# A gated attention and feed-forward block on one core: another order of the opening, the first maxima spread by TensorE, and small moves in the loop

## The chip, the cores and the metric

The kernel runs on 1 core of a Trainium2 chip. The metric is the device time of one execution, in microseconds (us); less is better.

## The reference

For each of 16 batches `x` is 256 x 512 and `ctx` 256 x 512. A gated attention with 8 heads of 64 is added to `x`, then a feed-forward part with quantised weights and activations:

```python
log_D = log_fg_matrix + ig.T                      # lower triangle, -inf elsewhere
max_log_D = jnp.max(log_D, axis=-1, keepdims=True)
D = jnp.exp(log_D - max_log_D)
C = (q @ (k.T / sqrt(DH))) * D
normalizer = jnp.maximum(jnp.abs(C.sum(-1, keepdims=True)), jnp.exp(-max_log_D))
h = C / (normalizer + EPS) @ v                    # then an RMS norm per head

def weight_quant(w):                              # one scale for a whole weight
    scale = 1.0 / jnp.clip(jnp.mean(jnp.abs(w)), EPS, None)
    return jnp.clip(jnp.round(w * scale), -1.0, 1.0) / scale

g, u = bitlinear(x, w_gate), bitlinear(x, w_up)   # 512 -> 2048
h = jnp.square(jax.nn.relu(g)) * u
return bitlinear(h, w_down)                       # 2048 -> 512

x = x + jnp.tanh(g_xattn[0]) * attention(layernorm(x), ctx, ctx, gates...)
x = x + jnp.tanh(g_ffn[0]) * ffn(layernorm(x), w_gate, w_up, w_down)
```

## The kernel before

Each engine has a program written out by hand, and they meet in semaphores. `step(b, n, m, par)` does the feed-forward part of batch b, the heads of batch n = b+1 and the gates of batch m = b+2; step 0 is written out, steps 1 to 12 run in a loop of two, and steps 13, 14 (no m) and 15 (no n) are written out too. In front of step 0 stands the opening: gates of batches 0 and 1, heads of batch 0, and the quantisation of the gate and up weights.

*Weights.* Each of `w_gate`, `w_up`, `w_down` comes as four pieces of 128 x 2048 (1 MB) into two buffers `stage`, gate and down in the first, up in the second. `magnitudes` (L506 on ScalarE, L739 on VectorE) sums a piece's absolute values, `weight_total` (L1077) and `weight_scale` (L729 to L734) make the scale `winv`, and `wprod` (L978, L980) the products of scales. Then a piece is multiplied and shifted by a magic number (L422 on GpSimd, L511 on ScalarE) and turned ternary, by a sign on ScalarE (L516) or by two roundings on VectorE (L745, L748). The down weight goes through all of this within step 0, the other two in the opening, where GpSimd scales all their pieces and VectorE rounds the four up pieces.

*Gates and maxima.* `gate_products` (L1164), `gates_in`, `forget_gate`, `log_forget` and `cumulative_sum` (L1174) give the sums; `cumulative` on VectorE writes `csum` and `a` (L842, L843); `a_rows` on TensorE transposes `a` (L1180), `running_max` scans it to `mrow` (L848). `spread_max` on SP stores `mrow` to memory (L358) and loads it back into `dmat`, on all 128 partitions (L364). `exponentials` on ScalarE work on `dmat` in place (L564, L570), `masks` on GpSimd (L429) cut the triangle, `scores` (L1124, L1125) and `weigh` on VectorE (L862) multiply, `heads_out` (L1137) gives the heads in the one bank `tp`, and `heads` on ScalarE (L578) copies each pair out.

*After the heads.* `normaliser` (L870 on), `head_squares` (L883), `mean_squares`, `head_rms`, `scale_heads` (L900), `residual` (L908, second half on GpSimd L436), `token_stats` (L915), `tokens_rstd`, `token_centres` (L925, L928), `quantise_tokens` (L935 to L945), `token_columns` on TensorE (L1198), `tokens` on ScalarE (L551).

*Feed-forward.* `chunk(b,t,c)` is the gate half (4 matmuls into `gb`) and the up half (4 into `ub`), L1090; `relu_square` L524 and L526; `hidden` on VectorE L755; `hidden_max` L762 and L767; `hidden_scale` L777 to L782; quantisation L788 and L544; `hidden_transposes` L1104; `hidden_cols` L538 and L796; `down` L1116 in two halves; `output` on VectorE L805. `keep_warm` (L1204) are matmuls whose result nobody reads.

In the loop TensorE runs `cumulative_sum`, the gate half of chunk (b,1,0), `a_rows`, and the up half; VectorE runs `scale_heads`, `output(b-1,1)`, `cumulative`, `residual`, `running_max`, `token_stats`, `hidden(b,1,0)`.

## Time and profile before

| | |
|---|---|
| three runs | 636.77, 637.5, 637.85 us; median 637.5 |
| the profiled execution | 638.38 us, of which span 636.7 us |
| mean granted TensorE clock | 0.965 |
| TensorE busy | 578.6 us (91%) |
| VectorE busy | 526.7 us (83%) |
| ScalarE busy | 454.3 us (71%) |
| GpSimd busy | 129.9 us (20%) |

The span runs from the first to the last instruction. In the rows PE is TensorE's matmuls, DVE VectorE, ACT ScalarE, POOL GpSimd and SPq the queue of SP, which only issues DMAs; L12 is line 12 of the kernel before. A timeline row is start, duration, engine, line, operation, output<-inputs, shapes and count, and in square brackets how long the engine had been idle and what released it. Rows are merged where an engine repeats.

### The profile page before, as it was taken

How to read it: one execution, taken by the hardware profiler on the slowest of the kernel's cores; microseconds unless marked ns; L12 is line 12 of the kernel's file. 1: busy time of each engine (PE TensorE's matmuls, PEld its weight loads, DVE VectorE, ACT ScalarE, POOL GpSimd, SP SyncE). 2: the span in 40 equal slices, each digit the busy share in tenths (PEclk: the TensorE clock that was granted, in tenths of full speed). 3: DMA queues.
4: the chain of work that ended last, by engine and by line, in shares of the span. 5: the costliest groups of instructions: out<-in, count | busy, mean ns of one | idle time of the engine just before them, and what ended most of it. 6: DMA issues, size and time to landing. Idle time of an engine off the chain costs nothing.

```text
span 636.7 us, 18420 instructions
## 1 busy us (share of the span) xinstructions
PE 578.6 (91%) x6596; PEld 338.0 (53%) x6596; DVE 526.7 (83%) x1144; ACT 454.3 (71%) x925; POOL 129.9 (20%) x266
## 2 busy tenths in 40 slices
PE   7592768999999999999999999999999999999896
PEld 4361443656555564656555565646565555656442
DVE  4479595898989989898989899898989899897964
ACT  5374979858685877858686868768586868677662
POOL 1256240212121202112121202021121212021200
PEclk9785968999999999999999999999999999999998
DMA  9884505041140505050320505050412305020000
GB/s 311 306 287 139 192 2 167 18 140 62 43 159 17 182 0 199 0 182 17 103 95 19 179 8 191 0 187 11 156 43 77 121 17 183 3 100 1 34 19 33
DMA packets 45169, 63.73 MB, mean 100 GB/s; under 512 B 1872, under 2 KB 26704, under 8 KB 45136
## 3 DMA queue, kind: packets, MB, share of 16 engines
q1 hardware_dynamic: 45136, 63.30, 28.8%
q8 instruction: 20, 0.33, 0.2%
q14 instruction: 13, 0.11, 0.1%
HBM read 54.77 MB, written 8.52 MB: 99 GB/s over the span
## 4 chain that ended last, share of the span: by engine, by line
PE 59%; DVE 17%; issue 10%; ACT 6%; DMA 5%; DVEq 1%; POOL 1%; SPq 0%; ACTq 0%; POOLq 0%
PE ub L1090 15%; PE gb L1090 14%; PE yb L1116 10%; PE ab L1124 6%; PE tp L1137 5%; PE ab L1104 3%; DVE ssq L883 3%; DMA stage<-in_w_up 2%; PE ab L1125 2%; DVE stage L805 2%; DMA xs<-in_x 2%; DVE stage L755 1%; DMA max_rows<-mrow 1%; PE ab L1198 1%; DVE dmat L862 1%
## 5 line engine op out<-in xcount | busy, mean ns | idle before, releaser
L1090 PE MATMUL ub<-wuT,xqT 128*128 128x512 bf16 x512 | 133.1, 383 | 2.0 <-DVE stage L755 2.0
L1090 PE MATMUL gb<-wgT,xqT 128*128 128x512 bf16 x512 | 133.3, 383 | 1.5 <-ACT xqT L551 1.5
L524 ACT ACTIVATE relu<-gb 128x512 f32<-128x512 f32 x128 | 75.4, 589 | 77.3 <-PE gb L1090 75.1
L1116 PE MATMUL yb<-wdT,stage 128*128 128x512 bf16 x512 | 122.8, 384 | 3.6 <-ACT stage L538 3.6
L755 DVE TENSOR_TENSOR stage<-relu,ub 128x512 f32<-128x512 f32 x128 | 87.0, 680 | 26.6 <-ACT relu L526 26.1
L862 DVE SCALAR_TENSOR_TENSOR dmat<-ab,dmat 128x384 f32<-128x384 f32 x128 | 65.3, 551 | 31.7 <-POOL dmat L429 22.7
L526 ACT ACTIVATE relu<-relu 128x512 f32<-128x512 f32 x128 | 80.7, 631 | 4.1
L1090 PEld LDWEIGHTS ub<-wuT,xqT 128*128 128x128 bf16 x512 | 50.3, 99 | 61.2 <-DVE stage L755 3.0
L1116 PEld LDWEIGHTS yb<-wdT,stage 128*128 128x128 bf16 x512 | 47.4, 99 | 53.4 <-issue 4.7
L1090 PEld LDWEIGHTS gb<-wgT,xqT 128*128 128x128 bf16 x512 | 46.0, 100 | 49.9 <-ACT xqT L551 1.8
L429 POOL TENSOR_SCALAR_AFFINE_SELECT dmat<-dmat 128x256 f32<-128x256 f32 x128 | 55.3, 461 | 68.0 <-ACT dmat L570 67.9
L1137 PE MATMUL tp<-values,dmat 128*64 128x65 f32 x1536 | 60.4, 229 | 3.6 <-issue 3.6
L1137 PEld LDWEIGHTS tp<-values,dmat 128*64 128x64 f32 x1536 | 51.5, 141 | 15.9 <-issue 10.8
L1124 PE MATMUL ab<-qT,cT 64*128 64x256 f32 x256 | 52.7, 437 | 5.4 <-DVE dmat L862 5.4
L570 ACT ACTIVATE dmat<-dmat,a 128x256 f32<-128x256 f32 x128 | 57.3, 496 | 0.0
L762 DVE TENSOR_REDUCE stage<-stage 128x1 f32<-128x1536 f32 x32 | 56.0, 1749 | 0.1
L459 POOL TENSOR_SCALAR dq<-hm,wprod 128x1 f32<-128x1 f32 x32 | 9.1, 284 | 222.8 <-DVE rhm L780 217.7
L564 ACT ACTIVATE dmat<-dmat,a 128x128 f32<-128x128 f32 x128 | 43.7, 391 | 7.0 <-DMA dmat<-max_rows 7.0
L436 POOL TENSOR_TENSOR x<-ysq,xs 128x512 f32<-128x512 f32 x16 | 28.4, 1774 | 82.4 <-DVE stage L805 78.3
L544 ACT ACTIVATE hq<-stage,hqs 128x1024 f16<-128x1024 f32 x32 | 36.7, 1146 | 5.7 <-DVE hqs L782 5.7
L578 ACT ACTIVATE ysb<-tp 128x260 f32<-128x260 f32 x64 | 24.5, 382 | 22.5 <-PE tp L1137 22.5
L1124 PEld LDWEIGHTS ab<-qT,cT 64*128 64x128 f32 x256 | 24.8, 188 | 26.5 <-issue 19.3
(110 smaller groups left out, 870.8 us busy)
## 6 DMA issues: line engine op xcount, KB each, us to landing
dmat<-max_rows SPq DMA_DIRECT2D x16, 1024.0 KB, 5.1
values<-in_ctx_v SPq DMA_DIRECT2D x16, 520.0 KB, 7.7
xs<-in_x SPq DMA_DIRECT2D x16, 512.0 KB, 5.9
cT<-in_ctx_t SPq DMA_DIRECT2D x16, 512.0 KB, 6.9
out<-stage SPq DMA_DIRECT2D x32, 256.0 KB, 2.0
stage<-in_w_gate SPq DMA_DIRECT2D x4, 1024.0 KB, 12.7
stage<-in_w_up SPq DMA_DIRECT2D x4, 1024.0 KB, 11.1
stage<-in_w_down SPq DMA_DIRECT2D x4, 1024.0 KB, 5.6
```

The costliest lines, as they stand in the source:

```text
L429: nc.gpsimd.affine_select(out=dv, in_=dv, compare_op=ALU.is_ge, fill=0.0, base=0, pattern=[[0, 2], [1, P]], channel_multiplier=-1).then_in ...
L524: nc.scalar.activation(relu[:, c % 2, :], gb[c % 2][:, :], ACT.Relu).then_inc(g_free, 1)
L526: nc.scalar.activation(relu[:, c % 2, :], relu[:, c % 2, :], ACT.Square).then_inc(r2_ready, 1)
L564: nc.scalar.activation(dmat[:, hd, 2, :], dmat[:, hd, 1, :], ACT.Exp, bias=a[npar][:, 1, hd:hd + 1], scale=-1.0).then_inc(e_low, 1)
L570: last = nc.scalar.activation(dh, dh, ACT.Exp, bias=a[npar][:, 0, hd:hd + 1], scale=-1.0)
L755: nc.vector.tensor_tensor(h[t][:, c * CH:(c + 1) * CH], relu[:, c % 2, :], ub[c % 2][:, :], ALU.mult).then_inc(h_done, 1)
L762: nc.vector.tensor_reduce(h[t][:, FF:FF + 1], h[t][:, 0:3 * CH], axis=AX_X, op=ALU.max, apply_absolute_value=True).then_inc(quant_step, 1)
L862: nc.vector.scalar_tensor_tensor(dh, ab[hd % 2][:, 0:3 * P], HD ** -0.5, dh, ALU.mult, ALU.mult).then_inc(a_free[hd % 2], 1)
L1090: last = nc.tensor.matmul(bank[c % 2][:, :], xqT[par][:, t, d, :], w[:, d, c * CH:(c + 1) * CH], start=(d == 0), stop=(d == KD - 1))
L1116: done = nc.tensor.matmul(yb[:, :], hqT[:, c, :], wdT[:, c, :], start=(c == 0), stop=(c == KF - 1))
L1124: nc.tensor.matmul(ab[e][:, 0:S], cT[npar][rows, kd, 0:P], qT[npar][rows, kd, 0:S], start=True, stop=True)
L1137: done = nc.tensor.matmul(tp[rows, (2 * t + e) * VW:(2 * t + e + 1) * VW], dmat[:, hd, block, rows], values[npar][:, s, hd, :], start=firs ...
```

## The change

*The opening.* The maxima of batch 0 no longer go through memory. A 0/1 matrix `pick` (8 x 1024, laid over a buffer that is free then) selects one row of `mrow` for each head, so that 8 matmuls `spread_max` write the rows on all partitions into the banks of `gb` and `ub`; ScalarE's `first_exponentials` read them there. The fillers of `keep_warm` go to `yb` for that time, and their counts change. The gates of batch 1 move behind the heads of batch 0 on TensorE, ScalarE and VectorE. SP's loads come in another order. `magnitudes` are dealt out anew between ScalarE and VectorE (gate pieces as before; up: ScalarE 0, 2 and 3; down: ScalarE 0 and 1, VectorE 2 and 3).

*Scaling.* GpSimd scales a piece in four instructions of 512 columns, all gate pieces (the third and fourth only after `wprod`) and down pieces 0 and 1. VectorE scales all up pieces and down pieces 2 and 3; ScalarE scales none. ScalarE makes up pieces 0 and 1 ternary by the sign, VectorE rounds pieces 2 and 3, now in step 0. Gate pieces 2 and 3 get their sign in step 0. The second residual half of batch 0 goes from GpSimd to VectorE.

*The loop.* On TensorE both halves of chunk (b,1,0) stand ahead of `a_rows`. On VectorE `cumulative` stands ahead of `output(b-1,1)`. In step 14 `hidden(b,1,0)` stands ahead of `token_stats`; in step 15 the fourth chunk stands ahead of the whole of `down`, and `output(b,0)` behind the last quantisation.

The diff, cut:

```diff
+        pick = hq[0][0:NH, :].bitcast(F32)
...
+        spread_rows = [gb[0], gb[1], ub[0], ub[1]]
...
-            for n in range(2):
-                keys(n, n)
-            weights(0, w_gate, 0, 4)
+            queries(0, 0)
+            keys(0, 0)
+            queries(1, 1)
+            weights(0, w_gate, 0, 2)
             padded_values(0, 0)
-            spread_max(0, 0)
+            weights(0, w_gate, 2, 4)
+            keys(1, 1)
             weights(1, w_up, 0, 4)
             padded_values(1, 1)
+            weights(2, w_down, 0, 1)
             spread_max(1, 1)
-            weights(2, w_down, 0, 4)
+            weights(2, w_down, 1, 2)
             load(2, 0)
+            weights(2, w_down, 2, 4)
...
 
                 gp.wait_ge(winv_step, WINV[m])
-                w = weight_piece(m, i)
-                nc.gpsimd.tensor_scalar(w, w, winv[:, m:m + 1], MAGIC32, ALU.mult, ALU.add).then_inc(w_scaled[m], 1)
+                for k in range(KD):
+                    w = weight_piece(m, i)[:, CH * k:CH * (k + 1)]
+                    last = nc.gpsimd.tensor_scalar(w, w, winv[:, m:m + 1], MAGIC32, ALU.mult, ALU.add)
+                last.then_inc(w_scaled[m], 1)
 
             def masks(n, p):
...
                 alone(gp, gp_passed)
                 nc.gpsimd.tensor_scalar(dq[:, t:t + 1], hm1[:, t:t + 1], wprod[:, 2:3], 0.0, ALU.mult, ALU.add).then_inc(dq_ready, 1)
 
+            for p in range(NP):
+                masks(0, p)
             scale_weight(0, 0)
-            masks(0, 0)
-            masks(0, 1)
             scale_weight(0, 1)
-            masks(0, 2)
-            masks(0, 3)
+            gp.wait_ge(winv_step, WINV[1] + 2)
             scale_weight(0, 2)
+            token_factor(0, 0)
             scale_weight(0, 3)
-            scale_weight(1, 0)
-            residual(0, 0)
-            for i in range(1, 4):
-                scale_weight(1, i)
-            token_factor(0, 0)
             masks(1, 0)
 
...
+            def first_exponentials(p):
+
+                act.wait_ge(rows_spread, p + 1)
+                for e in range(2):
+                    hd = 2 * p + e
+                    nc.scalar.activation(dmat[:, hd, 2, :], spread_rows[p][:, e * S + P:(e + 1) * S], ACT.Exp,
+                                         bias=a[0][:, 1, hd:hd + 1], scale=-1.0).then_inc(e_low, 1)
+                for e in range(2):
+                    hd = 2 * p + e
+                    last = nc.scalar.activation(dmat[:, hd, 0:2, :].rearrange("p c s -> p (c s)"),
+                                                spread_rows[p][:, e * S:(e + 1) * S], ACT.Exp,
+                                                bias=a[0][:, 0, hd:hd + 1], scale=-1.0)
+                last.then_inc(e_done, 1)
...
-            attention_rstd(1)
             forget_gate(0)
             magnitudes(0, 0, 0)
+            attention_rstd(1)
+            for p in range(NP):
+                first_exponentials(p)
+            heads(0, 0)
+            exp_minus_max(0, 0)
+            magnitudes(0, 2, 1)
+            for p in range(1, NP):
+                heads(0, p)
+            squares(0)
...
                     log_forget(m)
                 if n is not None:
                     scale_heads(n)
+                if m is not None:
+                    cumulative(m, par)
                 if prev:
                     output(b - 1, 1, npar)
-                if m is not None:
-                    cumulative(m, par)
                 if n is not None:
                     residual(n, npar)
                 if m is not None:
                     running_max(m, par)
+                else:
+                    hidden(b, 1, 0)
                 if n is not None:
                     token_stats(n, npar)
-                hidden(b, 1, 0)
+                if not prev:
+                    scale_weight(2, 2)
+                if m is not None:
+                    hidden(b, 1, 0)
                 if n is not None:
                     token_centres(n, npar)
+                if not prev:
+                    scale_weight(2, 3)
                 hidden(b, 1, 1)
...
-                output(b, 0, par)
+                if n is not None:
+                    output(b, 0, par)
                 hidden_scale(b, 1, par)
                 quantise_low(b, 1)
+                if n is None:
+                    output(b, 0, par)
...
-            def keep_warm(count):
+            def spread_max(p):
+
+                if p == 0:
+                    pe.wait_ge(tp_free, gate_use(0, A_ROWS) + 1)
+                for e in range(2):
+                    hd = 2 * p + e
+                    done = nc.tensor.matmul(spread_rows[p][:, e * S:(e + 1) * S], pick[:, hd * P:(hd + 1) * P], mrow[:, :],
+                                            start=True, stop=True)
+                done.then_inc(rows_spread, 1)
...
+            keep_warm(2, yb)
+            spread_max(0)
+            spread_max(1)
             scores(0, 0, 0)
             scores(0, 1, 0)
-            max_columns(1)
-            keep_warm(6)
-            weight_total(0)
+            spread_max(2)
+            spread_max(3)
+            max_columns(0)
+            keep_warm(1, yb)
...
-            keep_warm(6)
+            weight_total(0)
+            q_columns(1, 1)
+            gate_products(1, 1, 0, T * 2 * KD)
+            keep_warm(6, ub[1])
+            cumulative_sum(1)
+            a_rows(1, 1)
+            keep_warm(6, ub[1])
             weight_total(1)
-            keep_warm(24)
+            max_columns(1)
+            keep_warm(20, ub[1])
             token_columns(0)
...
-                chunk(b, 1, 0, par, 0, 1)
+                chunk(b, 1, 0, par)
                 if m is not None:
                     a_rows(m, par)
-                chunk(b, 1, 0, par, 1, 2)
                 chunk(b, 1, 1, par)
                 hidden_transposes(b, 0)
                 chunk(b, 1, 2, par)
                 if m is not None:
                     max_columns(m)
-                down(b, 0, 0, KF // 2)
-                chunk(b, 1, 3, par)
-                if n is not None:
+                if n is not None:
+                    down(b, 0, 0, KF // 2)
+                    chunk(b, 1, 3, par)
                     token_columns(n)
-                down(b, 0, KF // 2, KF)
+                    down(b, 0, KF // 2, KF)
+                else:
+                    chunk(b, 1, 3, par)
+                    down(b, 0, 0, KF)
```

TensorE in the loop, from `down` of the batch before to the second chunk, before:

```order
L1116 MATMUL yb<-wdT,stage 128x512 x8
...
L1174 MATMUL tp<-logf,upper 128x16
L1175 MATMUL tp<-logf,ones 128x8
...
L1090 MATMUL gb<-wgT,xqT 128x512 x4
...
L1180 MATMUL tp<-ident,a 8x128 x2
L1090 MATMUL ub<-wuT,xqT 128x512 x4
...
L1090 MATMUL gb<-wgT,xqT 128x512 x4
L1090 MATMUL ub<-wuT,xqT 128x512 x4
```

and in the change:

```order
L1181 MATMUL yb<-wdT,stage 128x512 x8
...
L1239 MATMUL tp<-logf,upper 128x16
L1240 MATMUL tp<-logf,ones 128x8
...
L1155 MATMUL gb<-wgT,xqT 128x512 x4
L1155 MATMUL ub<-wuT,xqT 128x512 x4
...
L1245 MATMUL tp<-ident,a 8x128 x2
...
L1155 MATMUL gb<-wgT,xqT 128x512 x4
L1155 MATMUL ub<-wuT,xqT 128x512 x4
```

The transposes of `a` moved from between the two halves of the chunk to behind them.

VectorE in the loop, from `scale_heads` (`ysq`) to the scan of the maxima (`mrow`), before:

```order
L900 TENSOR_TENSOR ysq<-ysb,scl 128x512 x2
...
L805 SCALAR_TENSOR_TENSOR stage<-yb,dq,x_0 128x512
...
L842 COPY csum<-tp 128x16
L843 TENSOR_TENSOR a<-gates,tp 128x16
...
L908 TENSOR_TENSOR x_0<-ysq,xs 128x512
...
L848 SCALAR_TENSOR_TENSOR mrow<-tp,zeros 8x256
L915 BN_STATS st<-x_0 128x6 x2
```

and in the change:

```order
L936 TENSOR_TENSOR ysq<-ysb,scl 128x512 x2
...
L878 COPY csum<-tp 128x16
L879 TENSOR_TENSOR a<-gates,tp 128x16
...
L835 SCALAR_TENSOR_TENSOR stage<-yb,dq,x_0 128x512
...
L944 TENSOR_TENSOR x_0<-ysq,xs 128x512
...
L884 SCALAR_TENSOR_TENSOR mrow<-tp,zeros 8x256
L951 BN_STATS st<-x_0 128x6 x2
...
L955 BN_AGGR mv<-st 128x2
```

`csum` and `a` moved ahead of the output (written to `stage`).

ScalarE in the opening, from the last pair of exponentials of batch 0 to the first sign of the gate weight, before:

```order
L564 ACTIVATE dmat<-dmat,a 128x128 x2
L570 ACTIVATE dmat<-dmat,a 128x256 x2
L506 ACTIVATE wdT,asum<-stage 128x2048
L578 ACTIVATE ysb<-tp 128x2x130 x2
L506 ACTIVATE wdT,asum<-stage 128x2048
L578 ACTIVATE ysb<-tp 128x2x130 x2
L591 ACTIVATE ysq<-ysb 128x512 x2
L516 ACTIVATE wgT<-stage,minus_magic 128x4x512
```

and in the change:

```order
L575 ACTIVATE dmat<-ub,a 128x128 x2
L579 ACTIVATE dmat<-ub,a 128x256 x2
L603 ACTIVATE ysb<-tp 128x2x130
L568 ACTIVATE enm<-negm 128x16
L519 ACTIVATE wdT,asum<-stage 128x2048
L603 ACTIVATE ysb<-tp 128x2x130 x3
L616 ACTIVATE ysq<-ysb 128x512 x2
L541 ACTIVATE qT<-ab 128x4x128 x2
L519 ACTIVATE wdT,asum<-stage 128x2048
L527 ACTIVATE wgT<-stage,minus_magic 128x4x512
```

The exponentials read the bank `ub`. One magnitude, not two, stands among the head copies (`ysb`), and the query copies `qT` of batch 1 and another magnitude stand between the squares and the sign.

## Rows read from the trace of the kernel before

**Rows 1.** Windows: span, then busy time (count) by engine, granted clock, DMA share, GB/s.

```profile
0.00:60.50 60.50, 36.62 (x490) 22.04 (x490) 38.68 (x74) 30.52 (x56) 25.45 (x37) 0.80 0.76 264
60.50:109.60 49.10, 37.52 (x378) 21.12 (x379) 33.89 (x72) 44.40 (x70) 10.86 (x16) 0.83 0.39 130
109.60:590.00 480.40, 466.40 (x5510) 276.05 (x5509) 423.75 (x947) 356.66 (x767) 89.89 (x205) 1.00 0.24 83
```

**Rows 2.** Windows: one step of the loop.

```profile
285.80:321.00 35.20, 34.18 (x410) 20.25 (x408) 31.25 (x71) 26.06 (x57) 6.62 (x15) 1.00 0.26 88
```

**Rows 3.** TensorE timeline, loop: start, us, instructions [idle before <-releaser].

```profile
308.44 1.02 PE L1090 MATMUL gb<-wgT,xqT 128*128 128x512 bf16 x4
310.38 0.38 PE L1180 MATMUL tp<-ident,a 128*8 128x128 f32 x2 [0.92 <-DVE a L843]
310.60 1.03 PE L1090 MATMUL ub<-wuT,xqT 128*128 128x512 bf16 x4
```

**Rows 4.** VectorE timeline, loop.

```profile
309.42 0.75 DVE L805 SCALAR_TENSOR_TENSOR stage<-yb,dq,x 128x512 f32<-128x512 f32 x1
310.08 0.17 DVE L842 COPY csum<-tp 128x16 f32<-128x16 f32 x1
310.16 0.16 DVE L843 TENSOR_TENSOR a<-gates,tp 128x16 f32<-128x16 f32 x1
```

**Rows 5.** ScalarE timeline, opening.

```profile
27.91 0.69 ACT L564 ACTIVATE dmat<-dmat,a 128x128 f32<-128x128 f32 x2 [6.99 <-DMA dmat<-max_rows]
...
40.87 0.39 ACT L578 ACTIVATE ysb<-tp 128x260 f32<-128x260 f32 x1 [1.06 <-PE tp L1137]
```

**Rows 6.** Windows: behind the heads, and the first step in two parts.

```profile
42.20:57.90 15.70, 5.61 (x27) 2.49 (x26) 14.62 (x32) 5.57 (x8) 10.24 (x8) 0.76 0.60 199
...
65.30:86.10 20.80, 15.42 (x207) 10.81 (x209) 13.09 (x32) 18.90 (x36) 3.38 (x8) 0.88 0.33 120
86.10:109.60 23.50, 17.33 (x170) 8.36 (x162) 16.10 (x35) 20.70 (x26) 6.57 (x8) 0.82 0.36 114
```

**Rows 7.** VectorE timeline, loop, the wait ahead of the third pair of weighings.

```profile
295.64 1.02 DVE L862 SCALAR_TENSOR_TENSOR dmat<-ab,dmat 128x384 f32<-128x384 f32 x2 [1.64 <-POOL dmat L429]
```

**Rows 8.** GpSimd timeline, loop.

```profile
310.25 1.81 POOL L436 TENSOR_TENSOR x<-ysq,xs 128x512 f32<-128x512 f32 x1 [5.54 <-DVE stage L805]
```

**Rows 9.** TensorE timeline, last two steps.

```profile
594.45 1.04 PE L1090 MATMUL ub<-wuT,xqT 128*128 128x512 bf16 x4 [1.82 <-DVE stage L755]
...
609.81 3.61 PE L1116 MATMUL yb<-wdT,stage 128*128 128x512 bf16 x16 [0.82 <-ACT stage L538]
...
626.89 1.71 PE L1104 MATMUL ab<-identh,hq 128*128 128x128 f16 x16 [2.22 <-DVE hq L788]
629.02 4.35 PE L1116 MATMUL yb<-wdT,stage 128*128 128x512 bf16 x16 [0.41 <-ACT stage L538]
```

**Rows 10.** TensorE timeline, first gate chunk.

```profile
60.53 1.89 PE L1090 MATMUL gb<-wgT,xqT 128*128 128x512 bf16 x4 [1.54 <-ACT xqT L551]
```

**Rows 11.** TensorE timeline, opening, two score heads.

```profile
20.55 0.71 PE L1124 MATMUL ab<-qT,cT 64*128 64x256 f32 x4
```

**Rows 12.** Groups, 0 to 110 us: shapes, count, busy us, mean ns, idle before.

```profile
L422 POOL TENSOR_SCALAR stage<-stage,winv 128x2048 f32<-128x2048 f32 x10 | 20.4, 2050 | 40.3 <-DVE winv L734 40.3
...
L739 DVE TENSOR_REDUCE asum<-stage 128x1 f32<-128x2048 f32 x4 | 9.1, 2281 | 2.0 <-DMA stage<-in_w_gate 1.0 <-DMA stage<-in_w_up 1.0
...
L745 DVE TENSOR_SCALAR wuT<-stage 128x2048 bf16<-128x2048 f32 x4 | 4.9, 1217 | 0.0
...
L516 ACT ACTIVATE wgT<-stage,minus_magic 128x2048 bf16<-128x2048 f32 x4 | 8.0, 1989 | 0.0
```

**Rows 13.** VectorE timeline, opening and first step.

```profile
45.39 1.85 DVE L980 TENSOR_TENSOR wprod<-wprod,wmean 128x1 f32<-128x1 f32 x1
...
51.54 3.37 DVE L925 TENSOR_SCALAR ysq<-x,mv 128x512 f32<-128x512 f32 x2
...
57.38 0.52 DVE L945 TENSOR_SCALAR xq<-ysq,qs 128x512 f16<-128x512 f32 x1
...
86.12 1.81 DVE L788 TENSOR_SCALAR hq<-stage,hqs 128x1024 f16<-128x1024 f32 x1
...
98.33 0.88 DVE L925 TENSOR_SCALAR ysq<-x,mv 128x512 f32<-128x512 f32 x2
```

More of the change, by code:

```diff
@@ L221, in bank_order @@
         def bank_order():
-            uses = [("column", 0, 0), ("column", 1, 0)] + [("score", 0, kd) for kd in range(KD)] + [("token", 0, 0)]
+            uses = [("column", 0, 0)] + [("score", 0, kd) for kd in range(KD)] + [("column", 1, 0), ("token", 0, 0)]
             for b, n, m in STEPS:
@@ L237, in row_order @@
         def row_order():
-            uses = [("gate", m, i) for m in range(2) for i in range(4)] + [("head", 0, p) for p in range(NP)]
+            uses = [("gate", 0, i) for i in range(4)] + [("head", 0, p) for p in range(NP)]
+            uses += [("gate", 1, i) for i in range(4)]
             for b, n, m in STEPS:
@@ L657, in step @@
                 if third:
-                    magnitudes(2, 0, 4)
+                    sign_weight(0, 2)
+                    exponentials(n, 1, npar)
                 if n is not None:
@@ L662, in step @@
                 if third:
-                    magnitudes(2, 1, 5)
+                    sign_weight(0, 3)
                 if n is not None:
@@ L671, in step @@
                 else:
[L672 removed]
+                    magnitudes(2, 0, 5)
                 relu_square(b, 0, 2)
@@ L816, in attention_stats @@
                     nc.vector.bn_aggr(mv[:, t, :], st[:, t, :]).then_inc(stat_step, 1)
+            def attention_stats(m, par):
+                for t in range(T):
+                    attention_sums(m, par, t)
+                attention_moments(m)
             def attention_norm(m, par):
@@ L1006, in step @@
                     weigh(n, 5)
+                if not prev:
+                    magnitudes(2, 2)
                 hidden(b, 0, 2)
@@ L1013, in step @@
                 hidden_max(b, 0, 0)
+                if not prev:
+                    magnitudes(2, 3)
                 hidden(b, 0, 3)
@@ L1083, in chunk @@
                     pe.wait_ge(a_free[t], token_use(b) + 1)
-                for bank, w, full, free, ready in ((gb, wgT, g_full, g_free, w_ready[0]), (ub, wuT, u_full, h_done, w_ready[1]))[first:last]:
+                for bank, w, full, free in ((gb, wgT, g_full, g_free), (ub, wuT, u_full, h_done))[first:last]:
                     if at(b, 0) and t == 0:
-                        pe.wait_ge(ready, c + 1)
+                        if w is wgT:
+                            pe.wait_ge(w_ready[0], c + 1)
+                        elif c < 2:
+                            pe.wait_ge(w_high, c + 1)
+                        else:
+                            pe.wait_ge(w_ready[1], c - 1)
                     if not (isinstance(k, int) and k < 2):
```

171 lines of the change are left out of this document (88 added, 83 removed).

## The prediction

> **What bounds the kernel now.** I read the windows first, to split the span: 60.5 us before the first feed-forward chunk, a first step of 49.1 us, and then a long even stretch [rows 1]. There one step takes 35.2 us, and TensorE is busy for 34.18 of it at clock 1.00, VectorE for 31.25, ScalarE for 26.06 [rows 2]. So TensorE binds the loop, with a hole of about 1 us per step. TensorE's timeline shows where: after the gate half of chunk (b,1,0) it waits 0.92 us for `a`, ahead of the transposes of `a_rows`; only then comes the up half [rows 3]. VectorE's timeline gives the reason: `output(b-1,1)`, 0.75 us, runs ahead of `csum` and `a` [rows 4].
>
> The opening is another matter. ScalarE waits 7.0 us for the maxima to come back by DMA and starts its exponentials at 27.9; the last head is copied at 40.9 [rows 5]. Behind the heads VectorE is the busy engine (14.62 of 15.7 us), and in the first step ScalarE (18.90 of 20.8 and 20.70 of 23.5) [rows 6].
>
> **Loop (steps 1 to 13).** `csum` and `a` go ahead of the output, which starts them 0.66 us earlier, and both halves of the chunk, 0.86 us more than one, go ahead of the transposes. `a` is then ready before TensorE asks, and the 0.92 us go, 13 times: 12.0 us at most. What is late next? I follow VectorE with a step of 34.3 us. Its list doesn't shrink, so at the first `weigh` of a step it lags TensorE by 0.9 us more than now. It catches up where it has slack, a wait of 1.64 us ahead of scores 4 and 5 [rows 7]. `weigh(n,1)` then ends about 0.2 us after TensorE wants scores 3. GpSimd's residual (1.81 us, [rows 8]) also waits for `output(b-1,1)`, now 0.24 us later, so the second token statistics wait 0.2 us; the hidden product (b,1,0) is still ready 0.1 us ahead of the up half of (b,1,2). The running maximum needs the transposes, done at about 310.6 on this clock, and VectorE reaches it at 310.9. I take 0.85 of the 0.92: **-11**, bounds -9.5 and -12. That it only changes places is a rival.
>
> **Last steps.** In step 14 a hidden product moves ahead of the token statistics and TensorE's wait of 1.82 us for it goes, but the `down` behind it needs `hidden_cols`, which on ScalarE stands behind `tokens_rstd` and so behind those statistics: about 0. In step 15 the last chunk no longer waits for half of `down`, until VectorE's maximum of three chunks sets the time: the last hidden product goes from 623.4 to 622.4. `output(15,0)`, 0.75, leaves the chain to the last quantisation. Together -1.8. TensorE idles 2.22 us there, after which 16 transposes take 1.71 and 16 `down` matmuls 4.35 us, against 3.61 for the same 16 after a hole of 0.82 [rows 9]. The hole shrinks to about 0.4 us, and I count 0.4 + 0.75 us more. **-3**, bounds -1 and -3.5.
>
> **Opening, up to the gate chunk now at 60.53** [rows 10]. The running maxima end at 14.3 as before. The spread is 8 matmuls of 256 columns, priced by the scores of the same width, 0.71 us a pair [rows 11]; only the first pair is on the path, so the exponentials start at 15.2 rather than 27.9. `pick` costs GpSimd a fill and a select of 1024 columns; GpSimd's 2048 columns take 2.05 us [rows 12], so the two take about 2.1 and end near 6, before TensorE's 16 warming matmuls: nothing, and up to 2 us if they are twice as slow. Among the heads ScalarE has one magnitude instead of two (about a sign's 1.99 us, [rows 12]), so the last head copy comes 12.7 + 2 earlier, at 26.2. The fillers stand where TensorE waits anyway. The normaliser starts a little later, at 26.4.
>
> From the normaliser to the quantised tokens (57.38) VectorE now takes 15.1 us. Added: magnitudes (1,1) 2.3; gates, sums and scan of batch 1, 1.5; a second weight scale 0.5; scaling up piece 0, 1.2 (priced by the rounding of as many elements); waits for ScalarE and a piece, about 1.4. Removed: 4.6 us that VectorE loses while GpSimd scales whole pieces, seen in a 1-element `wprod` of 1.85 us and two centrings of 3.37 us that take 0.88 later [rows 13]. GpSimd now idles until `wprod` is done. Net 17.4: tokens at 43.8. The 3.15 us from there to the chunk lose a sign that stood before the token copies, and gain 0.9 for the sign of up piece 0: chunk at 46.0, **14.5 early**.
>
> The stalls match the length of one GpSimd piece. The Trainium skill (GPSIMD Engine Reference, Key points) says that GpSimd shares its SBUF interfaces with VectorE, with contention for VectorE's two-port modes and two-input instructions; the trace agrees, with 1.85 and 3.37 us. By that rule the new overlap of quarters with VectorE's own scaling costs again; priced from the rows it is the second rival.
>
> **First step.** VectorE takes over two scalings (2.4), two roundings (3.8) and two magnitudes (4.6) [rows 12]. To its 13.09 busy us between the first `weigh` (65.3) and the first quantisation (86.1) that adds 10.8, with 1 us of waits 24.9. `weigh` starts at 50.3: 46.0, a sign 2.0, the rest of the token copies, a pair of exponentials 1.4, a mask pair 0.8. So the quantisation comes at 75.2 against 86.1. In the second half ScalarE loses two scalings (3.9 us, right ahead of relu (1,0)), and the quantisation, 1.81 us beside GpSimd [rows 13], shrinks towards 0.9. VectorE gets 2.4 us of scaling, and its scan can wait up to 1.8 us, because the transposes stand behind both chunk halves at the low clock. Net 21.5 instead of 23.5: step 1 starts at 96.7 instead of 109.6, 12.9 early. I take **-12**, since this walk gives VectorE no unplanned hole; bounds -6 and -16. The new load order costs nothing in it: a 1 MB piece lands each 2.7 to 3.3 us, so the last up piece, issued without the wait for the maxima, is there at 33 to 35, when ScalarE asks at 35.
>
> **Sum.** -11 - 3 - 12 = -26 against the profiled execution's 638.4 (span 636.7), so 612.4. That execution was 0.9 above the median of 637.5: **611.5 us**.
>
> **Rivals.**
> - *The loop's wait changes places.* VectorE is at 31.25 of 35.2, and the slacks above are a few tenths. If TensorE waits for `weigh` or a hidden product instead, -15 remains: 622.5. Against it: VectorE's own wait of 1.64 us per step. Chance 0.12.
> - *GpSimd's quarters hold VectorE.* Sixteen quarters of at least 0.5 us (2.05 / 4) run beside VectorE's scalings and both quantisations. If 10 VectorE operations on the path wait a whole quarter each, 5 us, and the tokens come 1 us later for it, the opening gives 6: 617.5. For it [rows 13]; against it, only half of the quarters stand beside a stretch in which VectorE binds. Chance 0.15.
> - *Slower, by the clock.* TensorE has a hole in each step now and a granted clock of 1.00. If the clock fell without the hole, 34.3 us of work would become 34.3/c. With 15 us gained outside, the kernel is slower than before once a step takes over 36.4 us, c under 0.94; at 0.9 a step is 38.1 and the time 660. No row of the loop shows it. Chance 0.03.
> - *The early exponentials don't come,* because the spread waits for a bank that something else holds: the opening gives 1, 622.5. The fillers ahead of it went to `yb`, so nothing should. Chance 0.02.
>
> **Numbers.** The forecast (0.68) spans 607 to 617. With the second rival the range is 606 to 620; outside it are the others, under 0.2. About 0.2% is what a measurement can tell from no change: faster 0.95, within it 0.01, slower 0.04.
>
> **What would show it.** Exponentials from about 15.2; the first gate chunk at 46, step 1 at 97; a step of 34.3 to 34.4 us and no wait of TensorE for `a`; the last 16 `down` matmuls in about 3.6 us. Wrong if a step stays at 35.2, if step 1 starts after 104, or if the loop's clock is under 1.00.

## The result, and the profile after

The changed kernel takes **613.2 us** (median of 4, 612.2 to 614.6) against 637.15 for the kernel before (median of 4, 636.77 to 637.85): ratio 0.9625, 95% interval 0.9601 to 0.9648. Forecast: 611.5, range 606 to 620. The profiled execution took 614.6, with a span of 612.9 at a mean granted clock of 0.974. The span splits like this (a step is taken from its first gate chunk to the next step's):

| part | before | changed | difference | predicted |
|---|---|---|---|---|
| start to step 1 | 109.6 | 102.9 | -6.7 | -12 |
| steps 1 to 13, each | 35.28 | 34.16 | -14.6 in all | -11 |
| step 14 | 32.73 | 32.73 | 0 | about 0 |
| step 15 to the end | 35.67 | 33.12 | -2.55 | -3 |
| sum | | | -23.8 | -26 |

**The loop.** TensorE's timeline of the changed kernel where [rows 3] had the hole (start, duration; line 1155 is the chunk, 1245 the transposition of `a`), and under it VectorE's:

```profile
329.82 1.02 PE L1155 MATMUL gb<-wgT,xqT 128*128 128x512 bf16 x4
330.68 1.03 PE L1155 MATMUL ub<-wuT,xqT 128*128 128x512 bf16 x4
331.54 0.38 PE L1245 MATMUL tp<-ident,a 128*8 128x128 f32 x2
331.76 1.03 PE L1155 MATMUL gb<-wgT,xqT 128*128 128x512 bf16 x4
```
```profile
330.81 0.17 DVE L878 COPY csum<-tp 128x16 f32<-128x16 f32 x1
330.89 0.16 DVE L879 TENSOR_TENSOR a<-gates,tp 128x16 f32<-128x16 f32 x1
```

`a` is written 0.5 us before TensorE asks for it, and TensorE no longer waits for VectorE there. The 35.28 us of the kernel before are an average: twelve of its 13 steps take 35.21 to 35.32 us, and one, step 2, takes 35.94. The regular step went from 35.22 to 34.15 or 34.17 us. From 102.9 to 547.1 the clock stays at its upper level and TensorE is busy for 435.7 of 444.2 us:

```profile
102.90:547.10 444.20, 435.70 (x5241) 264.15 (x5305) 404.31 (x911) 339.21 (x732) 83.86 (x195) 1.00 0.26 89
```

**The opening.** ScalarE's timeline of the changed kernel, against [rows 5]: the first exponentials, the third pair's, and the last head copy.

```profile
14.71 0.63 ACT L575 ACTIVATE dmat<-gb,a 128x128 f32<-128x128 f32 x2 [0.92 <-PE gb L1272]
...
20.00 0.63 ACT L575 ACTIVATE dmat<-ub,a 128x128 f32<-128x128 f32 x2 [2.23 <-PE ub L1272]
...
31.64 0.39 ACT L603 ACTIVATE ysb<-tp 128x260 f32<-128x260 f32 x1 [1.06 <-PE tp L1202]
```

They start 13.2 us earlier, but the last copy comes only 9.2 earlier. TensorE's timeline says why. Line 1272 is the spread, and the scores, 0.71 us in [rows 11], take 1.23 (x8 in a row of the spread is 4 matmuls, that is two pairs of heads, in two passes each):

```profile
13.53 2.86 PE L1272 MATMUL gb<-mrow,hq 8*128 8x256 f32 x8 [0.34 <-DVE mrow L884]
16.31 1.23 PE L1189 MATMUL ab<-qT,cT 64*128 64x256 f32 x4
17.32 0.64 PE L1190 MATMUL ab<-qT,cT 64*128 64x128 f32 x4
17.90 3.77 PE L1272 MATMUL ub<-mrow,hq 8*128 8x256 f32 x8
```

And the windows of the same stretch (busy us of TensorE, its weight load, VectorE, ScalarE, GpSimd; granted clock; DMA share; GB/s):

```profile
8.00:16.30 8.30, 6.93 (x123) 4.37 (x122) 5.43 (x14) 5.26 (x12) 0.06 (x1) 0.89 1.05 392
16.30:28.30 12.00, 12.00 (x84) 9.36 (x83) 4.03 (x8) 6.45 (x16) 3.01 (x8) 0.51 1.06 382
```

TensorE is busy for all 12.00 us there, at a clock of 0.51: the lower level, 1.2 GHz. What it did before the fall was the spread, passes of 8 rows. The profiled execution is also the slowest of the four, so -6.7 is the opening of one execution and not of the median.

**The end.** Step 14 has the new wait that the prediction named, 1.91 us for `hidden_cols`; the last hole is 0.62 us where [rows 9] had 2.22.

```profile
574.15 1.89 PE L1181 MATMUL yb<-wdT,stage 128*128 128x512 bf16 x8 [1.91 <-ACT stage L549]
...
604.04 1.07 PE L1169 MATMUL ab<-identh,hq 128*128 128x128 f16 x16 [0.62 <-DVE hq L818]
605.93 3.61 PE L1181 MATMUL yb<-wdT,stage 128*128 128x512 bf16 x16 [0.82 <-ACT stage L549]
```

### The profile page after: what moved, and what is told of

It is laid out like the page before. It is cut to its first block, busy times and chain, and to the rows that moved or that the text cites. A ratio compares the mean times of both kernels' runs of the same rounds, so it can differ in the third digit from the quotient of the medians.

```text
span 612.9 us, 18356 instructions
## 1 busy us (share of the span) xinstructions
PE 569.6 (93%) x6526; PEld 342.2 (56%) x6605; DVE 526.9 (86%) x1148; ACT 452.7 (74%) x923; POOL 125.9 (21%) x281
## 4 chain that ended last, share of the span: by engine, by line
PE 80%; DVE 10%; issue 5%; ACT 2%; POOL 2%; DMA 1%; SPq 0%; DVEq 0%; ACTq 0%; POOLq 0%
PE yb L1181 17%; PE gb L1155 16%; PE ub L1155 16%; PE tp L1202 8%; PE ab L1189 7%; PE ab L1169 4%; PE tp L1229 3%; PE ab L1212 2%; PE ab L1190 2%; POOL stage L439 1%; PE ab L1263 1%; DVE asum L763 1%; DVE stage L785 1%; DVE dmat L898 1%; DVE stage L770 1%
## 5 line engine op out<-in xcount | busy, mean ns | idle before, releaser
L1155 PE MATMUL ub<-wuT,xqT 128*128 128x512 bf16 x498 | 129.4, 381 | 2.5 <-DVE stage L785 1.7
L1155 PE MATMUL gb<-wgT,xqT 128*128 128x512 bf16 x479 | 127.1, 382 | 4.9 <-issue 4.1
L1181 PE MATMUL yb<-wdT,stage 128*128 128x512 bf16 x482 | 114.3, 379 | 6.6 <-ACT stage L549 3.5
L898 DVE SCALAR_TENSOR_TENSOR dmat<-ab,dmat 128x384 f32<-128x384 f32 x128 | 65.1, 549 | 25.8 <-POOL dmat L447 16.2
L1189 PE MATMUL ab<-qT,cT 64*128 64x256 f32 x256 | 54.4, 443 | 3.9 <-DVE dmat L898 3.9
L595 ACT ACTIVATE dmat<-dmat,a 128x256 f32<-128x256 f32 x120 | 53.7, 496 | 0.0
L454 POOL TENSOR_TENSOR x<-ysq,xs 128x512 f32<-128x512 f32 x15 | 24.7, 1646 | 79.6 <-DVE stage L835 79.6
L589 ACT ACTIVATE dmat<-dmat,a 128x128 f32<-128x128 f32 x120 | 41.0, 391 | 0.0
```

Of the source, the lines that this page charges most:

```text
L589: nc.scalar.activation(dmat[:, hd, 2, :], dmat[:, hd, 1, :], ACT.Exp, bias=a[npar][:, 1, hd:hd + 1], scale=-1.0).then_inc(e_low, 1)
L595: last = nc.scalar.activation(dh, dh, ACT.Exp, bias=a[npar][:, 0, hd:hd + 1], scale=-1.0)
L898: nc.vector.scalar_tensor_tensor(dh, ab[hd % 2][:, 0:3 * P], HD ** -0.5, dh, ALU.mult, ALU.mult).then_inc(a_free[hd % 2], 1)
L1155: last = nc.tensor.matmul(bank[c % 2][:, :], xqT[par][:, t, d, :], w[:, d, c * CH:(c + 1) * CH], start=(d == 0), stop=(d == KD - 1))
L1181: done = nc.tensor.matmul(yb[:, :], hqT[:, c, :], wdT[:, c, :], start=(c == 0), stop=(c == KF - 1))
L1189: nc.tensor.matmul(ab[e][:, 0:S], cT[npar][rows, kd, 0:P], qT[npar][rows, kd, 0:S], start=True, stop=True)
```

## The experiments

### 1 to 3: the loop's two orders, apart and together

```diff
 TensorE (pe_old, loop_old)
-                chunk(b, 1, 0, par)
+                chunk(b, 1, 0, par, 0, 1)
                 if m is not None:
                     a_rows(m, par)
+                chunk(b, 1, 0, par, 1, 2)
 VectorE (dve_old, loop_old)
-                if m is not None:
-                    cumulative(m, par)
                 if prev:
                     output(b - 1, 1, npar)
+                if m is not None:
+                    cumulative(m, par)
```

> This kernel is the changed one with both orders of the loop and of the steps around it put back: TensorE transposes a between the halves of the first down-product chunk, and VectorE runs the output's operations ahead of the cumulative sum. Theory (the loop's gain is the hole in front of the transposition of a, 1.08 us from start to start in each of 13 steps): the step goes back from 34.15 to about 35.3 us, the time to 613.2 + 14 = about 627 us, and the row of the transposition of a waits 0.9 us for VectorE again. Rival (part of the loop's gain comes from elsewhere, such as GpSimd's quarters or the unloaded queues): the time rises by 8 us or less.

> Only TensorE's order is put back (transposition of a between the halves of the chunk), VectorE keeps the new one. Theory (both streams had to move, since a needs some 0.5 us more VectorE work in front of it in one order than in the other, and TensorE arrives earlier by half a chunk): VectorE delivers a about 0.65 us sooner than before, so about 0.3 to 0.5 us of the wait stay in each of 13 steps, and the time is about 618 us (616 to 620). Rival (VectorE's order alone closes the hole): within 1 us of 613.2.

> Only VectorE's order is put back (output ahead of the cumulative sum), TensorE keeps the new one. Theory: TensorE now has the whole chunk to cover the wait, 0.85 us more than before, against a hole of 1.08 us, so 0.1 to 0.25 us stay in each of 13 steps: about 615.5 us (614.5 to 617). Rival (TensorE's order alone does all of it): 613.2 within 0.6 us, VectorE's move was worth nothing. Other rival (the eviction that the moved operations delay is what matters): over 618 us.

Measured: both back 625.1 us, TensorE's alone 617.6, VectorE's alone 615.4. The transposition of `a` in the profiles of loop_old, then of pe_old:

```profile
335.10 0.38 PE L1245 MATMUL tp<-ident,a 128*8 128x128 f32 x2 [0.91 <-DVE a L879]
```
```profile
331.50 0.38 PE L1245 MATMUL tp<-ident,a 128*8 128x128 f32 x2 [0.26 <-DVE a L879]
```

In dve_old its row carries no wait, but it starts 1.94 us after the gate half where the changed kernel has 1.72. The steps are 35.22, 34.56 and 34.36 us long; times 13, that is 13.8, 5.2 and 2.6 us over 34.16. Both moves are needed. Either one alone does most of the work, and what the last few tenths per step ask for is the other. With both back, the step is 35.22 us again, the regular step of the kernel before, so this hole is the whole gain per step, and the first rival (8 us or less) falls.

The times lie 0.4 to 1.9 us below these sums, and step 1 starts earlier in all three profiles (99.9, 100.9 and 101.7 instead of 102.9). Two things are in that. The first hidden quantisation comes at 79.7, 80.3 and 79.9 instead of 81.4, in code that is the same in all four up to there: experiment 4. And from it to step 1 it is 20.2 and 20.6 us with TensorE's old order, 21.6 and 21.8 without: experiment 5.

### 4: the spread over 128 rows

```diff
-                    done = nc.tensor.matmul(spread_rows[p][...], pick[:, hd * P:(hd + 1) * P], mrow[:, :],
+                    done = nc.tensor.matmul(spread_rows[p][...], pick[:, hd * P:(hd + 1) * P], mrow_all[:, :],
```

`pick` and `mrow_all` have 128 rows here; those behind the eighth hold zeros, for which GpSimd clears one more buffer.

> The one-hot spread of the maxima runs over 128 rows instead of 8: the picks are cleared on all 128 partitions and rows 8 to 127 of the maxima hold zeros, so that the products are the same and the matmuls have the shape 128x128 by 128x256. Theory A (the granted clock fell to 0.51 from 16.3 to 28.3 us because TensorE's work there, though it fills the time, is of few rows): the clock stays near 1.00 there, the passes fall from 0.36 to 0.47 us toward half, and the time falls by 3 to 5 us, to about 609. Theory B (the fall follows from something else ahead of it, such as the waits between 8 and 16 us where the granted clock was 0.89): the clock row still shows about 0.5 and the time is within 1 us of 613.2.

Measured: **609.8 us** (609.4 to 610.4), ratio 0.9563 (0.9528 to 0.9598). TensorE's timeline and the same windows as above:

```profile
14.04 1.99 PE L1274 MATMUL gb<-mrow,hq 128*128 128x256 f32 x8 [0.34 <-DVE mrow L886]
15.96 0.71 PE L1191 MATMUL ab<-qT,cT 64*128 64x256 f32 x4
...
16.82 1.99 PE L1274 MATMUL ub<-mrow,hq 128*128 128x256 f32 x8
```
```profile
8.00:16.30 8.30, 7.06 (x160) 4.82 (x162) 5.51 (x14) 4.89 (x12) 0.00 (x0) 1.00 1.05 390
16.30:28.30 12.00, 10.50 (x147) 8.77 (x144) 8.33 (x18) 8.77 (x23) 3.06 (x8) 0.98 1.06 381
```

Theory A holds. Sixteen times the array rows cost nothing per pass: in loop_old, where the clock fell a little later, eight 8-row passes also took 1.99 us. The fall itself is what costs, and it follows the few rows: in all seven profiles of kernels with the 8-row spread (the changed one, experiments 1 to 3 and 7 to 9) the clock fell before the second eight passes were done, and in all five with 128 rows it stayed at 0.98 to 1.00 from 16.3 to 28.3 us. From the first exponentials to the last head copy it is 11.1 us in each of the five, and 14.1 to 16.9 us in the seven, since the fall comes at another moment in each execution. The 16.9 are the changed kernel's. In loop_old, pe_old and dve_old the last head copy is 1.9, 1.0 and 1.3 us earlier than there, and the first hidden quantisation 1.7, 1.1 and 1.5. The last head copy is at 26.32 here; the prediction had 26.2.

The Trainium skill (TensorE: Matmul & The Clock Gate, Part 1) says that the clock follows how busy the engine has been. By that rule a stretch filled to 12.00 of 12.00 us should run at the upper level. These rows disagree, so the busy time that a profile shows does not tell the level by itself.

### 5: the old order in step 0 alone

On top of the 128-row spread, the first chunk of step 0 is split around `a_rows` again; the loop stays new. The reason is a wait in step 0 of the changed kernel. VectorE has `a` at 87.64, TensorE transposes it at 89.53, and the scan waits:

```profile
89.99 0.68 DVE L884 TENSOR_TENSOR_SCAN mrow<-tp,zeros 8x256 f32<-8x256 f32 x1 [1.59 <-PE tp L1245]
```

```diff
-                chunk(b, 1, 0, par)
+                chunk(b, 1, 0, par, 0, 2 if prev else 1)
                 if m is not None:
                     a_rows(m, par)
+                if not prev:
+                    chunk(b, 1, 0, par, 1, 2)
```

> The version with the 128-row spread, in which step 0 alone has TensorE's old order back (a transposed between the halves of the first chunk), and the loop keeps the new one. Theory: in step 0 VectorE has a ready 1.9 us before TensorE transposes it in the changed order, and VectorE's scan waits 1.59 us for that; with the old order in this one step the scan's wait goes and about 1 us comes back: 608.8 us (608 to 609.5). Rival (step 1 waits for something else by then, such as the tokens' activations on ScalarE): 609.8 within 0.4 us.

Measured: 608.2 us (607.6 to 609.1), ratio 0.9537 (0.9513 to 0.9561). Step 1 starts at 96.1 instead of 98.8. Of these 2.7 us, 1.0 lies ahead of the edit (the first hidden quantisation is at 76.0 instead of 77.1, in the same code); from that quantisation to step 1 are 20.0 us instead of 21.8, and the scan no longer waits. The changed kernel's variants with the old order in step 0 have 20.0 to 20.6 us there (warm_step0 of experiment 10, with its fillers, 21.3), and those with the new one 21.1 to 23.3. The timed gain over experiment 4, 1.6 us, is no larger than the intervals of the two ratios, so the traces are the better witness for it.

### 6: the first maxima through memory again

```diff
+            spread_max(0, 0)            (SP: store and load, behind keys(1, 1))
-            spread_max(0) ... spread_max(3)        (TensorE)
-                first_exponentials(p)
+                exponentials(0, p, 0)
```

> The first batch's maxima go through memory again, with one exponential over both halves as before; everything else is the changed kernel. Theory (the spread's gain is the wait of the first exponentials for the transfer, bought with about 6.6 us of TensorE passes in the same stretch, of which some 3 to 4 us lay on the path at the low clock): the first exponential starts about 6 us after the scan's end instead of 1.2, and the time rises by only 1 to 4 us over 613.2. Rival A (the exponentials' start was worth its full size): plus 6 us or more. Rival B (the spread as built costs all that it wins): within 1 us of 613.2 or faster.

Measured: 623.0 us, 9.7 more than the changed kernel. This expectation was wrong and rival A right. ScalarE's timeline and the waits of SP's queue:

```profile
27.88 0.69 ACT L591 ACTIVATE dmat<-dmat,a 128x128 f32<-128x128 f32 x2 [14.02 <-DMA dmat<-max_rows]
```
```profile
SPq L293 <- DMA max_rows<-mrow: 7.7, 1, 7.7
```

I had taken 6 us for the way through memory. ScalarE waits 14 here: SP stands 7.7 us for the 8 KB store while the queue moves weights, and the load takes another 5.2. The exponentials start at 27.9, as in the kernel before [rows 5]. There ScalarE waited only 7.0, because it had other work in front of them; SP waited 8.1 us for the same store, and the load took 5.0, so the trace of the kernel before already had the price that I put at 6. The spread is worth 9.7 us even with its clock, and 13 with 128 rows.

### 7: GpSimd's pieces whole

```diff
-                for k in range(KD):
-                    w = weight_piece(m, i)[:, CH * k:CH * (k + 1)]
-                    last = nc.gpsimd.tensor_scalar(w, w, winv[:, m:m + 1], MAGIC32, ALU.mult, ALU.add)
+                w = weight_piece(m, i)
+                last = nc.gpsimd.tensor_scalar(w, w, winv[:, m:m + 1], MAGIC32, ALU.mult, ALU.add)
```

> GpSimd scales each weight piece in one instruction of 2048 columns again instead of in four quarters; the pieces that VectorE took over stay with it. Theory (quarters let nothing start earlier than the whole piece, and each costs its own overhead; the weigh's wait of 4.25 us for GpSimd's mask follows the pieces): GpSimd's eight quarters of 5.39 us become about 4.6 to 5.4 us for two pieces, and the time is 613.2 within 1 us. Rival (the quarters shorten VectorE's or GpSimd's hold on the shared port): the time rises by over 1.5 us, and VectorE's rows beside the whole pieces are longer than the 1.28 us of the scaling row.

Measured: 613.7 us (612.7 to 615.0): no difference. GpSimd's timeline of the changed kernel, then of whole_pieces, for the first two gate pieces:

```profile
33.82 5.39 POOL L439 TENSOR_SCALAR stage<-stage,winv 128x512 f32<-128x512 f32 x8 [9.81 <-DVE winv L758]
```
```profile
31.02 3.93 POOL L438 TENSOR_SCALAR stage<-stage,winv 128x2048 f32<-128x2048 f32 x2 [8.91 <-DVE winv L757]
```

The two whole pieces take 3.93 us, less than the 4.6 to 5.4 that I expected. The quarters cost GpSimd 1.46 us for these two pieces and win nothing; the cost is hidden (from the last head copy to the first hidden quantisation it is 49.7 us with quarters and 49.8 with whole pieces). VectorE's scalings average 1.28 us beside whole pieces and 1.33 beside quarters.

### 8: two up pieces back to GpSimd

```diff
             scale_weight(0, 1)
-            gp.wait_ge(winv_step, WINV[1] + 2)
-            scale_weight(0, 2)
+            scale_weight(1, 0)
+            scale_weight(1, 1)
             token_factor(0, 0)
+            scale_weight(0, 2)
             scale_weight(0, 3)
```

VectorE loses `scale_weight(1, 0)` and `(1, 1)`.

> The changed kernel, but the scalings of the first two up pieces, (1,0) and (1,1), go back to GpSimd, ahead of its gate pieces (0,2) and (0,3); VectorE keeps the last two up pieces and everything else. Theory (GpSimd's mask, for which VectorE's first weighing waits 4.25 us, stands behind its weight pieces, so each piece given back delays the whole first step): four pieces at 2.7 us instead of two, the weighing starts about 3.5 to 5 us later, and the time is 617 to 618 us. Rival (VectorE is full there and gains the 2.9 us that it gives away, GpSimd's delay is hidden behind ScalarE's roundings): 613.2 within 1 us, or faster.

Measured: 616.1 us (615.5 to 616.4), 2.8 more. The mechanism is as expected and the size somewhat under it. VectorE's first weighing, in the changed kernel and in up_pool:

```profile
56.99 1.02 DVE L898 SCALAR_TENSOR_TENSOR dmat<-ab,dmat 128x384 f32<-128x384 f32 x2 [4.25 <-POOL dmat L447]
```
```profile
58.59 1.02 DVE L899 SCALAR_TENSOR_TENSOR dmat<-ab,dmat 128x384 f32<-128x384 f32 x2 [8.83 <-POOL dmat L447]
```

The two rows are only 1.6 us apart because the last head copy, ahead of the edit, came 1.2 us earlier in this execution (30.43 instead of 31.64). From that copy to the first weighing it is 28.2 us instead of 25.3. Moving the up pieces to VectorE is worth about 3 us, because GpSimd's mask for the next batch stands behind its pieces.

### 9: the last step's old orders

Half of `down(15, 0)` goes ahead of the last chunk on TensorE again, `output(15, 0)` ahead of the last magnitude row on VectorE.

> The last step has both old orders back (TensorE: half of the first down product ahead of the last chunk; VectorE: the output ahead of the last magnitude row), the rest is the changed kernel. Theory (2.55 us of the change came from the last steps, which lie on the chain to the end): 613.2 + 2.5 = 615.7 us (615 to 616.5). Rival (the end's gain was only the chain that the loop's shift made shorter): within 1 us of 613.2.

Measured: 615.3 us (613.8 to 616.2). Step 15 to the end takes 34.7 us against 33.1 in the changed kernel and 35.7 in the kernel before. The timed difference, 2.1 us, is inside the intervals of the two ratios. Against the changed kernel the orders are worth 1.6 us, so of the 2.55 us another 0.95 are not theirs. They are the clock:

```profile
603.26 1.07 PE L1166 MATMUL ab<-identh,hq 128*128 128x128 f16 x16 [2.22 <-DVE hq L818]
605.14 3.61 PE L1178 MATMUL yb<-wdT,stage 128*128 128x512 bf16 x16 [0.82 <-ACT stage L549]
```

The hole is 2.22 us, as in [rows 9], yet the transposes behind it take 1.07 and not 1.71. From the transposes to the end it is 9.8 us in the kernel before and 8.8 here. So the fall of the clock in that one execution did not follow from the hole's length alone, and about 1 us of the gain between the two profiles isn't the orders'. Over the transposes the granted clock is 0.57 in the kernel before, and 1.00 here.

### 10 and 11: fillers in step 0, and the length of a program

Experiment 5's version with fillers where TensorE waits in step 0:

```diff
+                    pe.wait_ge(g_free, 3)
+                    keep_warm(6, gb[0])
                     weight_total(2)
...
+                if not prev:
+                    keep_warm(8, gb[0])
                 if m is not None:
                     cumulative_sum(m)
```

> The version with the 128-row spread and step 0's old order, with fillers of 128x512 into a free bank at two places of step 0 where TensorE waits 2 to 3 us (6 ahead of the sum of the weight totals near 70 us, 8 ahead of the cumulative sum near 77 us). Theory (the granted clock of 0.83 from 80 to 90 us comes with the idle stretches just ahead, and the first chunk behind the cumulative sum, 1.87 us for 4 matmuls where the loop has 1.03, lies on the path): those rows show 1.03, and the time falls by about 1 us, to 607 (606.5 to 608). Rival (VectorE sets that stretch, TensorE's speed is covered): 608.2 within 0.5 us. Second rival (the fillers push the gate products back at the low clock): over 609 us.

Measured: 616.1 us, 8 more (five executions of 615.2 to 624.1; the profiled one took 632.5, and the others left no trace). That is far more than the second rival priced, and by another mechanism. The lines of its waits, its instruction loads from 105 to 590 us (packets, MB, share), and one place of the loop:

```profile
PE gb L1157 <- issue: 16.8, 3, 5.8
```
```profile
q8 instruction: 39, 0.64, 0.6%
```
```profile
172.00 1.89 PE L1157 MATMUL gb<-wgT,xqT 128*128 128x512 bf16 x4 [5.62 <-issue]
```

`issue` means that nothing the profile shows released the engine. Three steps, 3, 9 and 11, begin with such a wait of TensorE, 5.5 to 5.8 us; during each of them two blocks of instructions come in. In all, 39 blocks of 16 KB are loaded where experiment 5 has 13. With what follows each wait, the 13 steps take 23.2 us more than in experiment 5, nearly all of the 24.9 by which the two spans differ. That explains this execution; that the 8 us of the others are fewer such waits is likely and not shown. For the twin, 14 fillers were taken out of the opening:

```diff
             a_rows(1, 1)
-            keep_warm(6, ub[1])
             weight_total(1)
             max_columns(1)
-            keep_warm(20, ub[1])
+            keep_warm(12, ub[1])
```

> The version with the 14 fillers in step 0, and 14 fillers fewer in the opening (the 6 behind the second transposition of a, and 8 of the 20 ahead of the first tokens), so that TensorE's program is as long as in the version without the step 0 fillers. Theory A (the 616 us came from TensorE's program being reloaded in the loop: 39 instruction loads instead of 12 or 13 from 105 to 590 us, and waits of 5.5 to 5.8 us for issue at the start of a step, because the longer program puts the loop elsewhere in what is loaded at a time): the loads are back at 12 to 14, no wait for issue over 1 us stands in the loop, and the time is 608 to 610.5 us. Theory B (the fillers in step 0 cost by themselves, through the clock and the shifted first step): the time stays at 614 us or more with no reloads, or the reloads stay.

Measured: 608.3 us (607.1 to 609.6). The loads, and the window that the fillers were for, here and in experiment 5:

```profile
q8 instruction: 12, 0.20, 0.2%
```
```profile
80.00:90.00 10.00, 8.88 (x55) 4.33 (x55) 9.89 (x19) 9.38 (x11) 3.65 (x3) 1.00 0.42 148
```
```profile
80.00:90.00 10.00, 9.91 (x54) 4.85 (x55) 9.39 (x18) 9.67 (x12) 4.14 (x4) 0.83 0.38 114
```

So the fillers in step 0 do not cost the 8 us by themselves: a program of the old length has 12 loads and no such wait, with the fillers in the same place. In the three traces the time goes with the loads. And the clock from 80 to 90 us went from 0.83 to 1.00 without any gain, since VectorE, 9.89 of 10 us busy, sets that stretch: from the last head copy to step 1 it is 69.7 us in both. Why just this length makes the loop reload is open; no run varied it finely. The Trainium skill (Runtime: NRT & Kernel Launch, Instruction fetch mechanics) says that a taken branch to a target outside the loaded window has to fetch it first. The waits stand at the starts of steps 3, 9 and 11, where the loop of two steps has just branched back, which agrees.

### 12: gate activations ahead of the first rounding

```diff
             magnitudes(1, 0, 2)          (ScalarE)
-            sign_weight(0, 0)
             forget_gate(1)
             head_rms(0)
+            sign_weight(0, 0)
-            magnitudes(1, 1)             (VectorE)
             head_squares(0)
             gates_in(1)
             mean_squares(0)
+            magnitudes(1, 1)
```

> The version with the 128-row spread and step 0's old order, in which the second batch's gate activations on ScalarE come ahead of the first rounding (1.99 us), and VectorE's magnitude of one up piece (2.27 us) stands behind the mean squares instead of ahead of the head squares. Theory (VectorE stands 0.62 and 0.78 us in waits for those activations, at 33.2 and 34.0 us, and is full for the rest up to the first tokens): 1.4 us come back, 606.8 us (606.3 to 607.5). Rival (ScalarE's shifted rounding pushes its magnitudes and the second weight total back, so the up scalings start no earlier): 608.2 within 0.5 us.

Measured: **607.4 us** (606.3 to 608.5), ratio 0.9542 (0.9528 to 0.9556). In the profile step 1 starts at 94.8 instead of 96.1. That looks like the 1.4 us expected, but 0.5 of it is there before the edit: the last head copy comes at 25.8 instead of 26.3. From that copy to step 1 it is 69.0 us instead of 69.7, so the order is worth about 0.8 us, little more than half of what I expected. The timed difference to experiment 5 (0.7 us, and none in the ratio) is inside the intervals. The versions of experiments 4, 5 and 12 beat both kernels: by 28 to 30 us the one before, by 3.4 to 5.8 the changed one.

## Why the prediction was right, and where it was off

**Loop, -11 (measured -14.6).** The mechanism was right, the term mis-sized. I took the profile's 0.92 us for the hole, and 0.85 of it. From the start of the gate half to the start of the transposes the row pair says 310.38 - 308.44 = 1.94 us, where a half in a chain is 0.86 behind the one before: the hole is 1.08. The profile counts its idle time from a modelled end 0.16 us later. The 0.07 us that I kept for VectorE's lag did not show. The measured 1.12 us a step is over even my upper bound of 0.92. In the regular steps it is 1.06; the rest is the one long step 2 of the kernel before, 0.7 us, which loop_old, with both old orders, doesn't have. The rival of a wait that changes places fell; loop_old shows the hole to be all of the 1.06.

**Last steps, -3 (measured -2.6).** Step 14 is exactly the predicted zero, with the predicted wait. Of the rest 1.6 us are the orders (experiment 9), where I had 1.8. The other 1.15 I counted as the price of the 2.22 us hole in clock; tail_old has the hole without that price.

**Opening, -12 (measured -6.7).** The steps of the walk, predicted, measured and with the clock held (experiment 4):

| mark | predicted | changed | 128 rows |
|---|---|---|---|
| first exponentials | 15.2 | 14.7 | 15.2 |
| last head copy | 26.2 | 31.6 | 26.3 |
| normaliser | 26.4 | 32.4 | 27.1 |
| tokens quantised | 43.8 | 50.2 | 45.1 |
| first weighing | 50.3 | 57.0 | 51.8 |
| first hidden quantisation | 75.2 | 81.4 | 77.1 |
| step 1 | 96.7 | 102.9 | 98.8 |

One line failed: "The spread is 8 matmuls of 256 columns, priced by the scores of the same width, 0.71 us a pair [rows 11]; only the first pair is on the path". The scores' two heads use separate halves of the rows and run side by side (in experiment 4's trace two of their passes, 0.48 us each, lie within 0.49 us); the spread's passes follow one another, 1.0 us a pair at the upper clock. That alone is nearly free, as the third column shows. But its few rows brought the clock down, on a path on which heads and scores then took 1.6 to 1.7 times as long and the second half of the spread 1.9 times, and 5.4 us were lost by the last head copy. The kernel before also ran its first heads at the low clock (0.66 from 27.9 to 40.9 us), but there TensorE was busy for 9.1 of the 13.0 us and had room; in the changed kernel it is busy for 12.00 of 12.00. Every stretch after it came out within 0.6 us of the walk: 17.8 from normaliser to tokens (17.4), 24.4 from weighing to quantisation (24.9), 21.5 to step 1 (21.5, the scan's wait included). The stalls of VectorE that the walk took out are gone: the 1-element `wprod` operations take 0.16 us each, where one took 1.85.

**The rivals.** GpSimd's quarters do not hold VectorE at a price that counts: the stretches behind the head copy came out as walked, without the rival's 6 us, and whole pieces change nothing either (experiment 7). The loop's clock stayed at 1.00. The early exponentials came. The errors of the opening (5.3 us too much) and of the loop (3.6 too little) have opposite signs, so it is luck that the sum (-23.8 for -26) is nearer than these two terms; a fall of the clock stood only in the rival for the loop, not in the opening's walk.

## What to carry to other kernels

Measure a hole from start to start against a repeat of the same pattern without it; the idle time that a profile prints can be short by the modelled overlap, here 0.16 us a step, 2 us over 13 steps. Before you credit an edit with a mark that moved, compare a mark ahead of the edit. When matmuls over few rows are put on the path, look at the clock of what follows them: padding with zero rows gave back 3.4 us at no cost. And before adding instructions to a program with a loop, count its instruction loads: 14 matmuls more outside of the loop brought 8 us and long waits for instructions inside it, and none once 14 others were taken out.

## What the runs showed of the hardware

- Eight float32 matmul passes of 256 columns take 1.99 us over 8 rows as over 128. The granted clock went to 0.51 in 12 us that were fully busy, behind the 8-row passes, and stayed at 0.98 behind the 128-row ones, with 10.50 of 12.00 us busy. Up to 28.3 us it fell in all seven profiles with 8 rows and in none of the five with 128.
- The same hole of 2.22 us was followed by a slow stretch (1.71 us for 16 transposes) in one execution and by none (1.07) in another.
- SP waited 7.7 us for a store of 8 KB that it had issued among 1 MB loads running at 380 to 390 GB/s.
- With 14 more matmuls and their weight loads outside of the loop, instructions were loaded in 39 instead of 13 blocks between 105 and 590 us, and TensorE waited up to 5.8 us at a step's start; that kernel's executions took 615 to 632 us.
- GpSimd's scaling of 128x512 takes 0.67 us, of 128x2048 1.97: a quarter costs a third of the whole.
